# A fused graph network on one core: head one-hots stored once and loaded, and the message sums moved from GpSimd to VectorE

## The reference

```python
edge_index = jnp.stack([src, dst])
x = _layernorm(x + _L0_gnn_ref(x, L0_gnn_relation_emb, edge_index, edge_type_33), axis=-1)
x = _layernorm(x + _L1_gnn_ref(x, ...), axis=-1)   # two GRU rounds
x = _layernorm(x + _L2_gnn_ref(x, ...), axis=-1)   # two mean aggregations, hidden 16
x = _layernorm(x + _L3_gnn_ref(x, ...), axis=-1)   # two mean aggregations, hidden 128
```

```python
head_emb = entity_emb[head]; tail_emb = entity_emb[tail]; rel_emb = relation_emb[relation_type]
ricci = _l2_normalize(tail_emb + rel_emb)
hyper_head = expmap0(head_emb)
hyper_tail = expmap(tail_emb, hyper_head)
hyper_rel = expmap(rel_emb, hyper_head)
res = project(mobius_add(hyper_tail, hyper_rel))
res = logmap(res, hyper_head) + ricci * 1e-07
res = jax.nn.relu(res)
sums = jnp.zeros((n_entities, 64)).at[head].add(res)      # then divided by the counts
```

## Time and profile before

| | |
|---|---|
| median of 3 runs | 23582.91 us |
| the profiled execution's own time | 23574.29 us |
| its span | 23572.5 us |
| GpSimd busy | 16750.8 us (71%) |
| TensorE busy, weight loads | 11622.0 us (49%), 9627.6 us |
| VectorE busy | 9325.1 us (40%) |
| ScalarE busy | 2086.7 us (9%) |
| mean busy share of the 16 DMA engines, pass 0 | 23% |

### The profile page before, as it was taken

One profiled execution on the slowest core, in us unless ns is written; L12 is line 12 of the kernel. 1 busy time (PEld: TensorE's weight loads), 2 busy tenths in 40 slices (PEclk: granted clock), 3 DMA queues, 4 the chain that ended last, 5 costly groups with the idle time before them and its releaser, 6 DMA issues. The chain is left out here.

```text
span 23572.5 us, 203433 instructions
## 1 busy us (share of the span) xinstructions
PE 11622.0 (49%) x50453; PEld 9627.6 (41%) x50454; DVE 9325.1 (40%) x14116; ACT 2086.7 (9%) x3825; POOL 16750.8 (71%) x16828
## 2 busy tenths in 40 slices
PE   3232444577776777577763344334443334434343
PEld 1111222466665666466663333333333323333333
DVE  6555444588877888711121112111211121112112
ACT  0000101233322222200010001000000000000000
POOL 4777777777867777577747774777577767775776
PEclk6555656555555555555555555555555555555555
DMA  0000101122222222311121112111211121121112
GB/s 24 2 2 2 31 25 44 53 56 58 58 48 59 55 57 55 49 27 27 27 23 28 28 28 22 28 28 28 24 28 28 28 28 28 28 27 25 28 28 28
DMA packets 757921, 765.83 MB, mean 32 GB/s; under 512 B 444058, under 2 KB 524254, under 8 KB 737748
## 3 DMA queue, kind: packets, MB, share of 16 engines
q0 software_dynamic: 528384, 511.86, 13.8%
q1 hardware_dynamic: 229332, 251.96, 3.4%
HBM read 659.46 MB, written 103.37 MB: 32 GB/s over the span
## 5 line engine op out<-in xcount | busy, mean ns | idle before, releaser
L474 POOL DMA_INDIRECT rows<-table_lin,pay x9984 | 9443.9, 946 | 4164.0 <-issue 4106.2
L1558 DVE TENSOR_TENSOR acc<-acc,pair 128x1024 f32 x832 | 1015.9, 1221 | 10581.1 <-PE pair L723 10548.2
L723 PE MATMUL pair<-rows,onehot 128*128 128x64 f32 x19968 | 4800.1, 426 | 0.0
L723 PEld LDWEIGHTS pair<-rows,onehot 128*128 128x128 f32 x19968 | 4493.2, 332 | 520.7 <-issue 520.7
L711 PE MATMUL pair<-ones_bf,zeros_bf 1*128 1x512 bf16 x1664 | 838.4, 604 | 7675.8 <-issue 7670.2
L474 POOL DMA_INDIRECT rows<-table_hyp,pay x3328 | 3310.0, 995 | 1134.5 <-issue 998.8
L711 PEld LDWEIGHTS pair<-ones_bf,zeros_bf 1*128 1x128 bf16 x1664 | 109.2, 99 | 7805.2 <-issue 7805.2
L458 POOL DMA_INDIRECT payload_src<-rows x1600 | 1556.2, 973 | 737.9 <-issue 737.9
L686 PE MATMUL pair<-tab,sel_t 128*128 x6656 | 1575.4, 413 | 955.7 <-ACT xs L931 397.0
L458 POOL DMA_INDIRECT payload_dst<-rows x1600 | 1560.5, 975 | 499.1 <-issue 486.9
L686 PEld LDWEIGHTS pair<-tab,sel_t 128*128 128x128 f32 x6656 | 1380.0, 307 | 1242.9 <-issue 1242.9
(11 more groups left out here) (310 smaller groups left out, 14046.5 us busy)
## 6 DMA issues: line engine op xcount, KB each, us to landing
rows<-table_lin,pay POOLq DMA_INDIRECT x9984, 2.4
rel<-rel_rows SPq DMA_DIRECT2D x52, 1072.0 KB, 5.0
xs<-rel_rows SPq DMA_DIRECT2D x52, 1072.0 KB
rows<-table_hyp,pay POOLq DMA_INDIRECT x3328
rel_rows<-rel SPq DMA_DIRECT2D x26, 1072.0 KB, 4.1
rel_rows<-xs SPq DMA_DIRECT2D x26, 1072.0 KB
payload_src<-rows POOLq DMA_INDIRECT x1600, 2.1
payload_dst<-rows POOLq DMA_INDIRECT x1600
```

Source lines behind the costliest of these rows:

```text
L474: pool.indirect_dma_start(out=rows[:, h, t, 0:width], out_offset=None, in_=table[:, :], in_offset=bass.IndirectOffsetOnAxis(ap=pay[:, h, t ...
L723: last = nc.tensor.matmul(sums[:, bass.ds(at, D)], onehot[:, h, t, :], mv, start=False, stop=False, skip_group_check=True)
L1558: V.tensor_tensor(flat_acc[:, at], flat_acc[:, at], ps_half[u], ALU.add)
```

## The change

The head one-hots depend on the sorted list alone, and both hyperbolic passes use the same ones. The change makes them once, during the sort, stores them in HBM, and loads them in each pass in place of making them again. In the passes:

- VectorE makes the type one-hots only. It also adds the relation rows, per half, right behind its own addition of head and tail rows.
- GpSimd only multiplies the relation rows, in two halves. It does that for group g behind the 26th gather of group g + 1 (`MID`), in place of doing it behind the 32nd.
- SP loads a list once the gathers two groups before have landed, in place of once VectorE has freed the rows. It loads the relation rows once VectorE has added those of two groups before, and each half of one-hots once TensorE has summed with the half that it replaces.
- TensorE waits for the landing of the one-hots in place of VectorE's making them.

```diff
+MID = 26
...
+        head_hots = nc.dram_tensor("head_hots", (2 * GROUPS, P, HG * P), FP32, kind="Internal").ap()
...
+        hot_half = [flat_msg[:, 0:HG * P], flat_hot[:, 5900:5900 + HG * P]]
...
+            def store_hot(i, h, u):
+                await_reg(sp, "sp", types_made, 6 * i + (3 * h + u + 2))
+                sp.dma_start(head_hots[bass.ds(4 * i + (2 * h + u), 1)].rearrange("a q c -> (a q) c"), hot_half[u]).then_inc(hot_moved[h][u], 16)
+
+            def load_hot(m, i, h, u, free):
+                if free:
+                    await_reg(sp, "sp", scattered, 4 * i + (m * SUMMED + 2 * h + u - 3))
+                sp.dma_start(onehot[:, h, half(u), :].rearrange("p t n -> p (t n)"),
+                             head_hots[bass.ds(4 * i + (2 * h + u), 1)].rearrange("a q c -> (a q) c")).then_inc(hot_moved[h][u], 16)
...
             def types_pair(i, free):
                 for h in range(2):
                     if free:
-                        await_reg(sp, "sp", types_made, 2 * i + (h - 1))
+                        await_reg(sp, "sp", types_made, 6 * i + 3 * (h - 1))
                     load_pay(0, i, h)
+                for h in range(2):
+                    for u in range(2):
+                        store_hot(i, h, u)
                 for h in range(2):
                     store_rel(i, h)
...
                 with sp.Fori(1 if m < 2 else 0, ITERS) as i:
                     for h in range(2):
-                        await_reg(sp, "sp", rows_free, 2 * i + (m * FREE + h + 1))
+                        if m < 2:
+                            await_reg(sp, "sp", S["gathered", m][h], i * (G * 16))
+                            await_reg(sp, "sp", hot_made, 4 * i + (m * HOT + 2 * h - 2))
+                        else:
+                            await_reg(sp, "sp", rows_free, 2 * i + (m * FREE + h + 1))
                         load_pay(k, i, h)
                         if m < 2:
-                            await_reg(sp, "sp", S["mixed", m], MIXES * 2 * i + MIXES * (h - 1))
+                            await_reg(sp, "sp", S["coefficients", m], MIXES * 2 * i + MIXES * (h - 1))
                             load_rel(i, h)
+                            for u in range(2):
+                                load_hot(m, i, h, u, True)
...
             def mix(m, g, h):
-                hd, rl = head[h][:, :, 0:D], rel[h][:, :, 0:D]
-                await_reg(pool, "pool", S["coefficients", m], MIXES * g + 1)
-                nc.gpsimd.tensor_tensor(rl, rl, over(EO[:, 3, :], D), ALU.mult).then_inc(S["mixed", m], 1)
-                await_reg(pool, "pool", S["mixed", m], MIXES * g + 1)
                 for u in range(2):
-                    await_reg(pool, "pool", S["coefficients", m], MIXES * g + (u + 2))
-                    nc.gpsimd.tensor_tensor(hd[:, half(u), :], hd[:, half(u), :], rl[:, half(u), :], ALU.add).then_inc(S["mixed", m], 1)
+                    rl = rel[h][:, half(u), 0:D]
+                    if u == 0:
+                        await_reg(pool, "pool", S["coefficients", m], MIXES * g + 1)
+                    nc.gpsimd.tensor_tensor(rl, rl, over(EO[:, 3, half(u)], D), ALU.mult).then_inc(S["mixed", m], 1)
...
+                    def gather_and_mix(i, h, before_):
+                        gather(m, i, h, range(0, MID))
+                        mix(m, before_, 1 - h)
+                        gather(m, i, h, range(MID, G))
...
             def turn(m, i, h, q):
                 if q % (QG // 2) == 0:
-                    await_reg(pe, "pe", hot_made, 2 * g + (m * HOT + q // (QG // 2) + 1))
+                    await_reg(pe, "pe", hot_moved[h][q // (QG // 2)], 16 * i + ((m + 1) * LOADED + 16))
...
                         res = head[h][:, half(u), 0:D]
-                        await_reg(act, "act", S["mixed", m], MIXES * g + (u + 2))
+                        await_reg(act, "act", S["coefficients", m], MIXES * g + (u + 2))
...
                 dve.drain().then_inc(types_made, 1)
+                for u in range(2):
+                    for k in range(2):
+                        if k < h or turned:
+                            await_reg(dve, "dve", hot_moved[k][u], 16 * i + (16 if k < h else 0))
+                    V.tensor_tensor(hot_half[u].rearrange("p (t n) -> p t n", n=P), over(pay[:, h, half(u), 1], P),
+                                    ps_sort_iota.unsqueeze(1).to_broadcast([P, HG, P]), ALU.is_equal)
+                    dve.drain().then_inc(types_made, 1)
...
-                    TT(th, th, tr, ADD)
+                    ttl(th, th, tr, ADD)
+                    await_reg(dve, "dve", S["mixed", m], 2 * g + (u + 1))
+                    TT(th, th, rl[:, half(u), 0:D], ADD)
                     dve.drain().then_inc(S["coefficients", m], 1)
...
-                V.tensor_tensor(onehot[:, h, t, :], over(pay[:, h, t, 1], P),
-                                ps_iota.unsqueeze(1).to_broadcast([P, HG, P]), ALU.is_equal)
```

More of the change, by code:

```diff
@@ L216, in build @@
         rel_moved = [sem(f"rel_moved_{h}") for h in range(2)]
+        hot_moved = [[sem(f"hot_moved_{h}_{u}") for u in range(2)] for h in range(2)]
+        transposed, sel_copied = sem("transposed"), sem("sel_copied")
+        TURNS = GROUPS * QG
         types_made, types_turned, types_kept, rel_made, rel_kept = (
@@ L223, in build @@
             if n < 2:
-                for m in ("transposed", "sel_copied", "fetched", "fetch_copied", "asked", "answered", "coefficients", "mixed"):
+                for m in ("fetched", "fetch_copied", "asked", "answered", "coefficients", "mixed"):
                     S[m, n] = sem(f"{m}_{n}")
@@ L393, in _ @@
                 sp.wait_ge(rel_moved[h], LOADED)
+                for u in range(2):
+                    sp.wait_ge(hot_moved[h][u], LOADED)
             meet(sp, BN["prep0"])
@@ L465, in _, with gather @@
             meet(pool, BN["prep0"])
-            def gather(m, i, h):
+            def gather(m, i, h, tiles=range(G)):
                 table, width = (table_hyp, TW) if m < 2 else (table_lin, D)
-                await_reg(pool, "pool", loaded[h], 16 * i + ((m + 1) * LOADED + 16))
-                await_reg(pool, "pool", rows_free, 2 * i + (m * FREE + h + 1))
-                for t in range(G):
+                if tiles[0] == 0:
+                    await_reg(pool, "pool", loaded[h], 16 * i + ((m + 1) * LOADED + 16))
+                    await_reg(pool, "pool", rows_free, 2 * i + (m * FREE + h + 1))
+                for t in tiles:
                     pool.indirect_dma_start(
@@ L668, in _, with turn @@
             sum_regs = [pe.alloc_register(f"sum_block_{j}") for j in range(HG)]
-            def turn(m, g, h, q):
+            def turn(m, i, h, q):
+                g = 2 * i + h
                 if q % (QG // 2) == 0:
-                    await_reg(pe, "pe", hot_made, 2 * g + (m * HOT + q // (QG // 2) + 1))
+                    await_reg(pe, "pe", hot_moved[h][q // (QG // 2)], 16 * i + ((m + 1) * LOADED + 16))
                 if q > 1:
-                    await_reg(pe, "pe", S["sel_copied", m], g * QG + (q - 1))
+                    await_reg(pe, "pe", sel_copied, g * QG + (m * TURNS + q - 1))
                 for j in range(4):
                     last = nc.tensor.transpose(ps_sel[q % 2][:, j * P:j * P + P], onehot[:, h, 4 * q + j, :], ident[:, :])
-                last.then_inc(S["transposed", m], 1)
+                last.then_inc(transposed, 1)
             def fetch(m, g, h, q):
                 await_reg(pe, "pe", S["fetch_copied", m], g * QG + (q + 2))
-                await_reg(pe, "pe", S["sel_copied", m], g * QG + (q + 1))
+                await_reg(pe, "pe", sel_copied, g * QG + (m * TURNS + q + 1))
                 for j in range(4):
@@ L688, in fetch, with fetch_group @@
                 last.then_inc(S["fetched", m], 1)
-            def fetch_group(m, g, h):
-                turn(m, g, h, 0)
-                turn(m, g, h, 1)
+            def fetch_group(m, i, h):
+                g = 2 * i + h
+                turn(m, i, h, 0)
+                turn(m, i, h, 1)
                 for q in range(QG):
@@ L697, in fetch_group @@
                     if q + 2 < QG:
-                        turn(m, g, h, q + 2)
+                        turn(m, i, h, q + 2)
             def sum_group(m, g, h):
@@ L734, in run_pass @@
                     with pe.Fori(0, ITERS - 1) as i:
-                        fetch_group(m, 2 * i + 1, 1)
+                        fetch_group(m, i, 1)
                         sum_group(m, 2 * i, 0)
-                        fetch_group(m, 2 * i + 2, 0)
+                        fetch_group(m, i + 1, 0)
                         sum_group(m, 2 * i + 1, 1)
-                    fetch_group(m, GROUPS - 1, 1)
+                    fetch_group(m, ITERS - 1, 1)
                     sum_group(m, GROUPS - 2, 0)
```

13 lines of the change are left out of this document (6 added, 7 removed).

## The result

The changed kernel takes 23624.43 us (median of 14 runs, 23607.67 to 23627.38), the kernel before 23578.33 us (median of 14, 23560.39 to 23587.96). The ratio is 1.0019, with an interval of 1.0012 to 1.0027. The forecast was 23205 us with a range of 23090 to 23400: the change was to save 380 us and costs 46. What it left out is as large as what it counted.

The account below looks back on a forecast made before the run. Pass 0 was taken as bound by GpSimd's 40 + 10 us, pass 1 by VectorE with stalls. At 47.3 us per group, 130 + 233 + 17 (ends) = 380 us less gave 23194 profiled, stated as 23205, range 23090 to 23400.

Parts of the forecast that it names:

- c: In each group of the hyperbolic passes: the instant at which VectorE has the group's last coefficient.
- stretched gathers behind the product: GpSimd's six gathers after the relation product: 0.3 us added per group for stretching.
- ends of the passes: First and last groups of both passes: 17 us less in all, between 8 and 25.
- Start to c: VectorE, from a group's start to its last coefficient: 33.6 us after the change, from 40.97.
- c to the group's end: VectorE, from the last coefficient to the group's end: 11.8 us after the change, from 8.35.
- The preparation: Making and storing the head one-hots beside the scatters: taken as 0, with ends at 0 and 24 us.
- the head rows: Rows that ScalarE copies for line 1399: there at c + 8.25, in time for the start at c + 13.7.
- the slower rival: One-hot loads late in the passes: at 25 us landings 330 us more, 23910 us; chance 0.05.
- The new wait: VectorE's group start waits for six gathers behind the product: c + 13.7, period 47.3 us.
- The 3.92 us ahead of a group in pass 1: Late group start on VectorE before the change, read as lasting until GpSimd's additions end.
- The rule on shared SBUF interfaces: VectorE's two-input SBUF additions stretch GpSimd's gathers: period 51.0 us, 24 us less, 23559 us; chance 0.06 (no gain).
- The rows that the prediction called mixed: Pass 0 gathers before the change: one beside line 1403 took 1.86 instead of 0.94 us, one beside an addition 0.95.

Follow-up runs that it names:

- e1_rel_late: Changed kernel with one more wait on SP: the relation load waits until the next group's gathers have landed; 23340.48 us, 0.9899.
- e5_own_hots: Changed kernel, but VectorE makes the head one-hots in the passes again and none are loaded; 24058.50 us, 1.0203.
- e6_hots_only: Changed kernel, but GpSimd again multiplies and adds the relation rows behind its 32nd gather; stored one-hots and early lists stay; 23497.58 us, 0.9965.
- e12_no_adds: e1_rel_late without VectorE's two additions of the relation rows; 31489.01 us (0.9823), where the kernel before took 32039.94 us.
- its remedies: e1_rel_late's wait, MID = 27, gathered rows freed behind their last addition, and empty drains ahead of both passes (32 and 64); 31063.19 us, 0.9828.

## Why the prediction was wrong, step by step

**The step that failed is one sentence:** "The relation load, the list load, now a group earlier, and these share SP's queue: each wait in it is for an event earlier in the cycle than the need behind it, so I cost them at nothing." It asked of each load only whether it comes in time for its own user. The diff moves the wait of the relation load from GpSimd's `mixed` to VectorE's `coefficients`, and so its issue to c + 12, just between the last gather's start (c + 10.4) and the landing of the rows (c + 13.7), as the forecast had them. It also had c + 12.2 for the moment at which VectorE is done with the group, and never laid the load's issue beside the other two. It even cited that all queues share the engines, and gave the rule no price. In the kernel before, the load is issued as the first of a group's 32 gathers starts (5606.94 and 5606.87 us), and VectorE takes these rows some 47 us later. e1_rel_late prices it: 2.9 us per group, 278 us.

The miss is 23618.6 - 23194 = 425 us on the profiled execution:

| term of the sum | forecast | measured | 96 groups |
|---|---|---|---|
| relation load in the way | 0 | 2.9 us | 278 us |
| stretched gathers behind the product | 0.3 us | 0.85 + 0.22 + 0.24 = 1.3 us | 1.0 x 96 = 96 us |
| turn of VectorE's loop, every second group | 0 | 0.8 us | 0.8 x 48 = 38 us |
| ends of the passes | 17 us less | 0 | 17 us |

That is 429 us, and the stages behind the passes came out 5 us shorter. The second and third terms are read in e1_rel_late, where the first is gone: there VectorE starts at c + 14.7 on average, and where its loop turns at c + 15.5. In the changed kernel it starts at c + 17.8 and c + 18.3, so the turn is at least in part hidden there.

**Right.** Start to c was to be 33.6 us, and is 33.2 to 33.6 in pass 0 and 33.2 to 34.1 in pass 1. c to the group's end was to be 11.8 us and is 11.8. GpSimd starts the product 0.2 us after c. The preparation cost nothing. No start waited for the head rows, each for the gathered rows. The one-hots were not late (e5_own_hots), so the slower rival named the wrong load: the mechanism "a DMA is late" was right, and its place was not. The new wait was for the six gathers, as forecast, only it was over at c + 18.1 on average in place of c + 13.7. With the collision out of the way the periods are 48.6 and 48.8 for the 47.3 forecast, and 23340 us lie within the range given; but that is another kernel than the one forecast.

**Wrong in reading.** The 3.92 us ahead of a group in pass 1 were put down to GpSimd's additions. Pass 1 of the kernel before has 120 instruction transfers and 3.9 us at every turn of VectorE's loop; pass 0 has 2 and 1.2 us. That this is what makes pass 1 slower there was not tried by shifting that kernel, and in e6_hots_only, where GpSimd is the bound, a pass with transfers is as fast as one without. The row said "issue", not GpSimd.

**Right in kind, wrong in size.** The rule on shared SBUF interfaces was given 3.7 us for four additions and a chance of 0.06. The gathers beside them are stretched by 1.3 us in all, and taking away two of the four gave 0.4. The rows that the prediction called mixed agree with each other: the gather at 5046.91 was not stretched since it started ahead of the addition. The 0.3 us in its sum were too little by the 1.0 us above.

## What to carry to other kernels

When a change moves what a load waits for, ask not only whether it still arrives in time, but what is in flight when it starts: write down the issue times of all DMAs of one cycle, and keep a bulk load off the last few microseconds before the landing of a small transfer that something waits for. Here one more wait on SP was worth 1.2%. A start marked "issue" on every second turn of a loop is worth a look at the queue of instruction transfers, and where the code lies may explain two passes that do the same work at different speeds.

## What was unexpected in the hardware

- A 1072 KB load on SP's queue left no packet to GpSimd's gathers for 2.8 us (106 packets, 87.8% of the 16 engines), though the gathers had been issued before or beside it. Half the load cost 60% as much.
- A GpSimd gather that starts while a VectorE instruction with two SBUF inputs runs takes until 0.80 to 0.87 us after that instruction's end, whatever is left of it: 1.15 to 3.09 us in place of 0.94 in the changed kernel.
- The turn of one and the same VectorE loop took 3.6, 7.7 or 1.4 us, with its code shifted by 32, 64 or 96 instructions; with 1.4 us the instruction queue was silent.
- In three runs everything took a third longer, the kernel before 31607.78 or 32039.94 us. Gathers issue as fast (0.95 us each); in e12_no_adds a group takes 20 us more, and ScalarE, VectorE and TensorE show one long stop in it. There the changed kernel gains 1.5% (0.9851), and with its remedies 1.7% (0.9828).
